# A causal mask moved from TensorE matmuls to a GpSimd select, and normalisation moved ahead of the low halves in two later stages of a two-layer transformer kernel

## The chip, the cores and the metric

One core of one Trainium2 chip runs the whole program in one launch. The metric is device microseconds (us) from start to end of an execution. The profile comes from one more execution under the hardware profiler. Engines are named as the profile names them: PE is TensorE's matmuls, PEld its weight loads, DVE is VectorE, ACT ScalarE, POOL GpSimd, SP SyncE.

## What is computed

```python
h = layernorm(x) * (1 + ca) + sa
x = x + ga * causal_attention(h)      # B=2, T=2048, C=256, 16 heads of 16, 32 rotary dimensions, softmax over keys <= query
h = layernorm(x) * (1 + cb) + sb
x = x + gb * experts(h)               # 8 experts of 3 layers; softmax over tokens, the 2 largest of 8
h = layernorm(x) * (1 + ca1) + sa1
z = softmax(h @ W_A.T * 0.25, over tokens)
x = x + ga1 * ((toeplitz(z) @ v) @ W_O + b_O)  # out[i] = sum over j <= i of z[i - j] * v[j], for each head
h = layernorm(x) * (1 + cb1) + sb1
x = x + gb1 * sigmoid(xr @ W_r) * (relu(xk @ W_k)**2 @ W_v)   # xr, xk mix a token with the one before it
```

All inputs and the output are float32; the scale and shift vectors come from a small conditioning product.

## The kernel before

Six stages follow one another with a barrier between them: start (projections), attention, route, experts, mix and tail. `N` = 8 chunks of 512 tokens, `NB` = 2 batches of `NCH` = 4 chunks. Each engine has its own instruction list, written by hand, and engines meet at semaphores alone.

**Attention** (`phase_attention`) runs 8 units `u` (4 groups of 4 heads, times 2 batches). A unit has 40 steps: for each chunk `qc` of 512 queries, in the order 3, 2, 1, 0 (unit 0: 2, 3, 1, 0), all blocks `kb` of 128 keys up to the diagonal. In the last four steps of a chunk the key block lies on the diagonal, at `t = kb - 4*qc` = 0 to 3, and the query columns shrink to 512, 384, 256 and 128. Of the 40 steps 16 are diagonal. In a step PE does, for each of two head pairs `f`, six score matmuls of half the array's rows each (two at a time, lines L916 and L920), and on a diagonal step four more of 128 columns (L925) that add -1e30 to the future keys of the block, as mask times identity in bf16. ACT takes the exponential (L963) into one of two buffers `pr`. PE then multiplies the step before with the values (`weighted`, L898); it waits there for `exp_done` of both `f`:

```python
for s in range(NS):
    ahead(u, s, 0)
    ...
    scores(s, 0)
    scores(s, 1)
    ...
        weighted(grp, b, s - 1)
    ahead(u, s, 7)
```

**Maxima.** The softmax's shift is the true row maximum, found in advance: PE computes the score products a second time, transposed (`maxima`, L863), into three banks used as a ring; DVE reduces each (L999, on the diagonal L996, with a mask of its own) and frees the bank. When a chunk of queries is done, its maxima are gathered (DVE L1006), turned by PE (L874), scaled by DVE (L1010), and sent by four DMAs of the SP queue (L837) into the row of `sqk` that scores of that chunk read (`shift_ld`). `schedule()` decides at build time at which place of which step (0 to 7) each maximum and each turn is issued: it plays the steps through with a cost in ns for each operation, among them 106 ns for the mask of each `f`, and holds maxima back until it takes a bank to be free. At place 0 of a chunk's first step it puts as many maxima as fit until 5400 ns (`FETCH`) after that chunk's turn.

POOL in attention first splits the experts' weights into f16 high and low parts (24 times: fetch L771, L784, L787, store L790), then stores each finished chunk (L799), fills zeros (L803), loads and stores the sums' inverses.

**Route** (`phase_route`): for each chunk PE projects the attention output (L1354), DVE adds it to `x` (L1176), takes statistics (L1183, L1187), ACT the root (L94), DVE normalises (L1197), PE transposes (L1364), ACT modulates (L1307), PE computes gate logits (L1388) and transposes back (L1395), ACT copies the f16 high halves (L1332), DVE subtracts for the low halves (L1204, `low`). **Mix** (`phase_mix`) has the same flow (DVE add L1723, statistics, normalise L1744, low halves L1752; PE transposes L1853, products for `z` L1862 and `v` L1870). It then takes the softmax of `z` over tokens (DVE maximum L1757, ACT exponential L1802), POOL scales it and splits it into f16 halves (L1679, L1683, L1685, 16 partitions of 2048), SP stores it and reads it back as Toeplitz tiles (L1713), and 32 units of matmuls follow (L1899, L1901). In both stages PE's list for chunk n is: outputs of n + 2, transposes of n + 1, products of n.

## Time and profile before

| | us |
|---|---|
| median of 3 runs (range) | 1815.13 (1814.72 to 1819.74) |
| profiled execution: time, span of its instructions | 1819.15, 1817.5 |
| PE, DVE, ACT, POOL busy | 1551.9, 1154.6, 893.4, 362.4 |
| attention, from 192.1 to 1048.9 | 856.8 |
| route up to the softmax, from 1064.0 to 1158.8 | 94.8 |
| mix up to its first unit, from 1472.0 to 1560.5 | 88.5 |

Busy times are unions of an engine's instructions; a granted clock of 1.00 is TensorE's full 2.4 GHz. The rows by stretch further down are those of attention, route, mix and, last, of attention's unit 3 alone. The profiled execution took 4.0 us more than the median. Averages over the span mix six stages, so a change is read in its own stage.

### The profile page before, as it was taken

What the parts mean: (1) busy time and instruction counts of PE and PEld (TensorE: products, weight loads), DVE (VectorE), ACT (ScalarE), POOL (GpSimd) and SP (SyncE); (2) the same over time, 40 slices, a digit from 0 to 9 for tenths busy, and PEclk for the clock granted to TensorE, in tenths of its full rate; (3) what the DMA queues carried; (4) which work ended last, traced back from release to release, by engine and by line L of the source; (5) the groups of instructions that cost most, each with busy time, mean ns of one, the idle gap of its engine ahead of it and who ended that gap; (6) DMA issues with size and microseconds to landing.
All of it is one profiled execution on the core that took longest, in us unless ns stands there. A gap on an engine that the chain in (4) does not pass through costs nothing. (4 is left out here: it accounts for less than half of the span.)

```text
span 1817.5 us, 34523 instructions
## 1 busy us (share of the span) xinstructions
PE 1551.9 (85%) x13070; PEld 851.3 (47%) x13070; DVE 1154.6 (64%) x3222; ACT 893.4 (49%) x1272; POOL 362.4 (20%) x432
## 2 busy tenths in 40 slices
PE   7994989999999999999999958401899967988898
PEld 5451334444444434444343334200787744666776
DVE  3746888888888888888888138400556666211775
ACT  2430456666666666666666714300676734201443
POOL 2471782000000000000000022175111001510011
PEclk9995889999999999999999989655999979999999
DMA  8378442304040130404010045024777600776011
GB/s 301 110 215 207 137 134 77 66 29 86 17 95 5 45 70 29 86 15 93 8 42 15 30 148 205 16 106 94 89 82 78 77 7 2 245 282 231 12 35 47
DMA packets 102197, 166.59 MB, mean 92 GB/s; under 512 B 23596, under 2 KB 72492, under 8 KB 100884
## 3 DMA queue, kind: packets, MB, share of 16 engines
q1 hardware_dynamic: 83124, 113.15, 26.6%
q0 software_dynamic: 16112, 47.59, 8.3%
q10 hardware_dynamic: 2800, 3.64, 0.6%
q8 instruction: 109, 1.79, 0.5%
q14 instruction: 52, 0.43, 0.1%
HBM read 107.76 MB, written 56.47 MB: 90 GB/s over the span
## 5 line engine op out<-in xcount | busy, mean ns | idle before, releaser
L963 ACT ACTIVATE at_pr<-ps 128x1024 f32<-128x1024 f32 (+3 forms) x640 | 542.5, 894 | 296.6 <-PE ps L920 175.9
L999 DVE TENSOR_REDUCE at_mx<-ps 128x1 f32<-128x512 f32 x768 | 483.2, 684 | 87.2 <-PE ps L863 84.1
L920 PE MATMUL ps<-bq,bk 64*128 64x512 f16 (+3 forms) x1280 | 287.1, 346 | 0.0
L996 DVE CUSTOM_DVE_ANT_0 at_seen<-ps,later 128x384 bf16<-128x384 f32 (+3 forms) x512 | 228.4, 487 | 20.6 <-PE ps L863 18.9
L916 PE MATMUL ps<-sqk 64*128 64x512 f16 (+3 forms) x1280 | 215.3, 348 | 0.1
L916 PE MATMUL ps<-at_sqk 64*128 64x512 f16 (+3 forms) x1280 | 207.5, 345 | 0.5 <-ACT at_pr L963 0.2
L863 PE MATMUL ps<-sqk 64*128 64x512 f16 (+3 forms) x640 | 173.8, 375 | 22.7 <-PEq L543 11.4
L863 PE MATMUL ps<-at_sqk 64*128 64x512 f16 (+3 forms) x640 | 157.9, 350 | 1.1 <-DVE at_mx L999 0.7
L898 PE MATMUL ps<-at_pr,at_vl 128*32 128x512 f32 (+3 forms) x1280 | 150.0, 541 | 0.1
L898 PE MATMUL ps<-at_pr,vl 128*32 128x512 f32 (+3 forms) x1280 | 150.0, 541 | 0.0
L863 PEld LDWEIGHTS ps<-sqk 64*128 64x128 f16 x640 | 45.5, 94 | 164.9 <-DVE at_mx L999 89.6
L920 PEld LDWEIGHTS ps<-bq,bk 64*128 64x128 f16 x1280 | 98.4, 94 | 39.6 <-issue 0.2
L1517 PE MATMUL ps<-ex_id,ex_xr 128*128 128x128 f16 x312 | 25.5, 228 | 105.7 <-DMA ex_xr<-d_rows 104.8
L1899 PE MATMUL ps<-mi_vhl,mi_tz 128*128 128x512 f16 (+15 forms) x512 | 96.0, 284 | 15.5 <-DMA mi_tz<-d_z 15.4
L1541 PE MATMUL ps<-ex_hh,exw 128*128 128x256 f16 x624 | 105.2, 274 | 0.9 <-DVE ex_hl L1597 0.9
L863 PEld LDWEIGHTS ps<-at_sqk 64*128 64x128 f16 x640 | 42.9, 93 | 132.8 <-DVE at_mx L999 70.4
L916 PEld LDWEIGHTS ps<-at_sqk 64*128 64x128 f16 x1280 | 77.0, 94 | 54.0 <-ACT at_pr L963 23.0
L916 PEld LDWEIGHTS ps<-sqk 64*128 64x128 f16 x1280 | 82.8, 95 | 40.4 <-ACT at_pr L963 8.2
L925 PE MATMUL ps<-mask,ident 64*128 64x128 bf16 x1024 | 95.9, 216 | 0.0
L1557 ACT ACTIVATE ex_xt<-ps 128x1024 f16<-128x1024 f16 x39 | 40.0, 1025 | 103.2 <-PE ps L1517 102.9
L1901 PE MATMUL ps<-mi_vhl,mi_tz 128*128 128x256 f16 (+15 forms) x512 | 87.8, 225 | 0.0
L1541 PE MATMUL ps<-ex_hl,exw 128*128 128x256 f16 x312 | 85.3, 274 | 0.1
(277 smaller groups left out, 2351.2 us busy)
## 6 DMA issues: line engine op xcount, KB each, us to landing
mi_tz<-d_z SPq DMA_DIRECT2D x32, 1024.0 KB, 7.1
ex_xr<-d_rows SPq DMA_DIRECT2D x39, 256.0 KB, 8.7
d_rows<-at_nil POOLq DMA_DIRECT2D x31, 322.0 KB
d_va<-st_va SPq DMA_DIRECT2D x8, 1024.0 KB, 4.3
d_o<-at_oc POOLq DMA_DIRECT2D x32, 256.0 KB, 2.4
at_pw<-in_w POOLq DMA_DIRECT2D x24, 256.0 KB, 3.3
d_w<-at_ph POOLq DMA_DIRECT2D x24, 256.0 KB, 2.4
exw<-d_w SPq DMA_DIRECT2D x8, 768.0 KB, 13.5
```

Source lines behind the costliest of these rows:

```text
L863: pe.matmul(ps[:, MAXB + slot % RING, 0:hi_ - lo], g.sqk[b][half[r], 0, i, 0, qb * P:(qb + 1) * P], g.sqk[b][half[r], 1, i, 0, lo:hi_], st ...
L898: ins = pe.matmul(ps[32 * h:32 * h + 32, O, off:CH], g.vl[b][:, kb, 32 * h:32 * h + 32], pr[:, n % 2, h // 2, h % 2, off:CH], start=(kb == 0),
L916: pe.matmul(ps[:, 2 * f + r, off:CH], g.sqk[b][half[r], 1, f, part, k], g.sqk[b][half[r], 0, f, part, q], start=part == 0, stop=False)
L920: ins = pe.matmul(ps[:, 2 * f + r, off:CH], g.bk[half[r], b, k], g.bq[half[r], b, q], start=False, stop=t < 0)
L925: ins = pe.matmul(ps[:, 2 * f + r, off:off + P], g.ident2[half[r], m, :], g.mask2[half[r], m, :], start=False, stop=m == 1)
L963: act.activation(pr[:, n % 2, f, :, off:CH], ps[:, 2 * f:2 * f + 2, off:CH], ACT.Exp, scale=INV_SCALE).then_inc(exp_done[f], 1)
L996: ins = dve.tensor_tensor_reduce(seen[:, turn, r, 0:n], src, g.later[:, CH - n:CH], 1.0, LOWEST, ALU.add, ALU.max, dst)
L999: ins = dve.tensor_reduce(dst, src, AX.X, ALU.max)
L1541: ins = pe.matmul(out(l, cc)[:, o, :], lhs, rhs, start=(i == 0), stop=(i == len(parts) - 1))
L1557: act.activation(xt[:, cc % 2], turning(cc), ACT.Copy).then_inc(xt_ready, 1)
L1899: pe.matmul(out[:, :, d * HD:C], tz[:, x, 0, w], vhl[:, :, tiles, h * HD:(h + 1) * HD], start=(d == 0), stop=False)
L1901: ins = pe.matmul(out[:, 0, d * HD:C], tz[:, x, 1, w], vhl[:, 0, tiles, h * HD:(h + 1) * HD], start=False, stop=(d == NT - 1))
```

## The change

It has three parts.

1. **Attention.** The mask matmuls go. The exponential runs on unmasked scores, and POOL then sets the future keys of each diagonal block of `pr` to zero by `affine_select` (128 partitions x 2 x 128), one for each `f`: 256 in all. `weighted` waits for `masked` on diagonal steps. POOL's list is rewritten around that: the weight splits are spread over the chunks of units 0 to 2 (`SPLITS`), zeros are filled in the long chunks, stores of a chunk come early in the next. The planner loses its 106 ns entries, and so its table changes. The constants `mask2` and `ident2`, their loads and their casts in the start stage go.
2. **Route and mix.** `normalise(n + 2)` stands ahead of `low(n)` in DVE's list.
3. **Mix.** The maximum of `z` is taken chunk by chunk; `Z_SCALE` goes into the sum; ACT instead of POOL writes the high halves, beside POOL's scaling.

```diff
-            pool.dma_start(msk32[:, :, :], g.i["mask2"]).then_inc(late_ld, 16)
-            pool.dma_start(idn32[:, :, :], g.i["ident2"]).then_inc(late_ld, 16)
...
-                dve.tensor_copy(g.gb0[:, 1, :], craw[0:VROWS, 0, 1, 1, :])
-                dve.wait_ge(late_ld, 16 * (NLATE + 1))
-                dve.tensor_copy(g.ident2[:, :, :], idn32[:, :, :])
-                dve.tensor_copy(g.mask2[:, :, :], msk32[:, :, :]).then_inc(gate_used, 1)
+                dve.tensor_copy(g.gb0[:, 1, :], craw[0:VROWS, 0, 1, 1, :]).then_inc(gate_used, 1)
...
-    INV_STEP = 24
+    INV_STEP = 14
+    SPLITS = {(0, 2): 6, (0, 3): 7, (0, 1): 2, (1, 3): 4, (1, 2): 3, (2, 3): 2}
...
-                        if i % 3 == 0 and t >= 0:
-                            rows[:] = [max(rows) + 106] * 2
...
-            pool.wait_ge(ld[1], loaded(0, 1))
-            fetch(0)
-            for n in range(3 * E):
+            def split(n):
...
+            def store(u, i):
+                grp, b = divmod(u, NB)
+                qc = ORDER[u][i]
+                pool.wait_ge(out_moved, u * NCH + i + 2)
+                pool.dma_start(g.d_o[grp][:, b * T + qc * CH:b * T + (qc + 1) * CH], oc[:, i % 2, :])\
+                    .then_inc(o_stored[i % 2], 16)
+
...
+            def mask_step(u, n, t):
+                d = u * NS + n
+                cut = slice(t * P, (t + 1) * P)
+                for f in range(2):
+                    pool.wait_ge(exp_done[f], d + 2)
+                    block_ = pr[:, n % 2, f, :, cut]
+                    pool.affine_select(block_, block_, pattern=[[0, 2], [1, P]], compare_op=ALU.is_ge, fill=nought, base=0,
+                                       channel_multiplier=-1).then_inc(masked[f], 1)
+
+            pool.wait_ge(ld[1], loaded(0, 1))
+            fetch(0)
+            n_split = 0
+            nought = pool.to_reg(0.0)
+
             def body(grp, b, last):
+                nonlocal n_split
                 u = index(grp, b)
                 for i, qc in enumerate(ORDER[u]):
-                    pool.wait_ge(out_moved, u * NCH + i + 2)
...
+                    if qc and (u or i):
+                        store(*divmod(u * NCH + i - 1, NCH))
+                    if i == 0 and u:
+                        load_sums(u - 1)
+                    if i == 1 and u:
+                        store_inverses(u - 1)
+                    if qc:
+                        for x in range(1 + (qc == 3)):
+                            fill(u * NCH + sum(1 + (q == 3) for q in ORDER[u][:i] if q) + x)
+                    for n in range(SPLITS.get((u, qc), 0)):
+                        split(n_split)
+                        n_split += 1
+                    for t in range(TPC):
+                        mask_step(u, ENDS[u][qc] - TPC + 1 + t, t)
+                        if qc == 0 and t == 0:
+                            store(u, i - 1)
+                if last:
+                    store(u, NCH - 1)
...
-                    pe.wait_ge(exp_done[f], u * NS + n + 2)
+                    if kb >= TPC * qc:
+                        pe.wait_ge(masked[f], u * NT + diagonals(u, n) + 1)
+                    else:
+                        pe.wait_ge(exp_done[f], u * NS + n + 2)
...
-                                        start=False, stop=t < 0)
-                    if t >= 0:
-                        for m in range(2):
-                            for r in range(2):
-                                ins = pe.matmul(ps[:, 2 * f + r, off:off + P], g.ident2[half[r], m, :],
-                                                g.mask2[half[r], m, :], start=False, stop=m == 1)
+                                        start=False, stop=True)
...
                     add(n + 2)
                     statistics(n + 2)
+                    normalise(n + 2)
                 low(n)
-                if n + 2 < N:
-                    normalise(n + 2)
...
-                pool.tensor_scalar(z[:, b, :], z[:, b, :], zrec[:, b:b + 1], Z_SCALE, ALU.mult, ALU.mult).then_inc(zn_ready, 1)
-                pool.wait_ge(zn_ready, b + 1)
                 if b:
                     pool.wait_ge(z_st[b - 1], 32)
-                pool.tensor_copy(zhl[:, 0, :], z[:, b, :]).then_inc(zh_ready, 1)
+                pool.tensor_scalar(zn[:, :], z[:, b, :], zrec[:, b:b + 1], None, ALU.mult).then_inc(zn_ready, 1)
+                pool.wait_ge(zn_ready, b + 1)
                 pool.wait_ge(zh_ready, b + 1)
-                pool.tensor_tensor(zhl[:, 1, :], z[:, b, :], zhl[:, 0, :], ALU.subtract).then_inc(zl_ready, 1)
+                pool.tensor_tensor(zhl[:, 1, :], zn[:, :], zhl[:, 0, :], ALU.subtract).then_inc(zl_ready, 1)
...
-            def largest(b):
-                dve.wait_ge(z_ready, NCH * (b + 1))
-                dve.tensor_reduce(nmax[:, b:b + 1], z[:, b, :], AX.X, ALU.max, negate=True).then_inc(nmax_ready, 1)
+            def largest(n):
+                b, it = n // NCH, n % NCH
+                dve.wait_ge(z_ready, n + 1)
+                dve.tensor_reduce(zmax[:, b, it:it + 1], z[:, b, it * CH:(it + 1) * CH], AX.X, ALU.max).then_inc(zmax_ready, 1)
+                if it == NCH - 1:
+                    dve.wait_ge(zmax_ready, n + 1)
+                    dve.tensor_reduce(nmax[:, b:b + 1], zmax[:, b, :], AX.X, ALU.max, negate=True).then_inc(nmax_ready, 1)
 
             def inverse(b):
                 dve.wait_ge(exp_ready, b + 1)
+                dve.tensor_scalar(zsum[:, b:b + 1], zsum[:, b:b + 1], 1.0 / Z_SCALE, None, ALU.mult).then_inc(sum_ready, 1)
+                dve.wait_ge(sum_ready, b + 1)
                 dve.reciprocal(zrec[:, b:b + 1], zsum[:, b:b + 1]).then_inc(rec_ready, 1)
...
                 if n + 2 < N:
                     add(n + 2)
                     statistics(n + 2)
+                    normalise(n + 2)
                 low(n)
-                if n + 2 < N:
-                    normalise(n + 2)
-                if n == NCH - 1:
-                    largest(0)
+                largest(n)
                 if n == NCH:
                     inverse(0)
-            largest(1)
             inverse(1)
...
+            def highs(b):
+                act.wait_ge(rec_ready, b + 1)
+                if b:
+                    act.wait_ge(z_st[b - 1], 32)
+                act.activation(zhl[:, 0, :], z[:, b, :], ACT.Copy, scale=zrec[:, b:b + 1]).then_inc(zh_ready, 1)
...
                     exps(0)
+                    highs(0)
             exps(1)
+            highs(1)
```

How the table moves. PE's list (`L863`, after the change `L897`, are maxima; `L874`/`L908` the turn; `L916`/`L953` and `L920`/`L957` the scores; `L925` the mask; `L898`/`L935` the values). Before, at the end of unit 1, from the turn of unit 2's first chunk (first row) to that chunk's first scores (last row):

```order
L874 MATMUL ps<-ident,at_mm 128x128
L863 MATMUL ps<-sqk 128x512 x2
L916 MATMUL ps<-at_sqk 128x384 x4
L920 MATMUL ps<-bq,bk 128x384 x2
L925 MATMUL ps<-mask,ident 128x128 x4
L863 MATMUL ps<-sqk 128x512
...
L925 MATMUL ps<-mask,ident 128x128 x4
L863 MATMUL ps<-sqk 128x128
L898 MATMUL ps<-at_pr,at_vl 32x256 x4
L916 MATMUL ps<-sqk 128x512 x2
```

The same place after the change, again from the turn (second row) to the first scores (last row):

```order
L953 MATMUL ps<-at_sqk 128x256 x2
L908 MATMUL ps<-ident,at_mm 128x128
L897 MATMUL ps<-sqk 128x512 x2
L953 MATMUL ps<-at_sqk 128x256 x2
...
L897 MATMUL ps<-sqk 128x512 x2
L953 MATMUL ps<-at_sqk 128x128 x4
...
L935 MATMUL ps<-at_pr,at_vl 32x256 x4
L897 MATMUL ps<-sqk 128x128 x2
L897 MATMUL ps<-sqk 128x512 x4
L897 MATMUL ps<-sqk 128x128 x2
L953 MATMUL ps<-sqk 128x512 x2
```

The turn stood in front of step 37; it now stands inside step 38, behind half of its first scores. Between it and the next unit's first scores lay the rest of three steps (37 to 39) and 12 maxima, spread out among them; now it is the rest of two, and 12 maxima, eight of them in one piece directly ahead of those scores.

DVE's list in route, before:

```order
L1187 BN_AGGR ro_mv<-ro_st 128x2 x4
L1204 TENSOR_TENSOR ro_rows<-ps,ro_rows 128x4x256
L1193 RECIPROCAL ro_rs<-ro_sd 128x4
L1197 TENSOR_SCALAR ro_hn<-x,ro_mv,ro_rs 128x256 x4
L1228 TENSOR_REDUCE ro_cmax<-ro_lg 8x1
```

and after:

```order
L1219 BN_AGGR ro_mv<-ro_st 128x2 x4
L1225 RECIPROCAL ro_rs<-ro_sd 128x4
L1229 TENSOR_SCALAR ro_hn<-x,ro_mv,ro_rs 128x256 x4
L1236 TENSOR_TENSOR ro_rows<-ps,ro_rows 128x4x256
L1259 TENSOR_REDUCE ro_cmax<-ro_lg 8x1
```

The subtraction (L1204, now L1236) has changed places with the reciprocal and the four normalisations.

## Rows read from the trace of the kernel before


**Rows 1.** The page's costliest groups, line L925: out<-in, times, busy us and mean ns, idle

```profile
L925 PE MATMUL ps<-mask,ident 64*128 64x128 bf16 x1024 | 95.9, 216 | 0.0
```

**Rows 2.** Stretch, its us, busy PE, PEld, DVE, ACT, POOL, granted clock, DMA share, GB/s

```profile
192.10:1048.90 856.80, 848.42 (x8676) 349.85 (x8676) 685.69 (x2033) 557.50 (x673) 123.26 (x168) 0.99 0.23 56
1064.00:1158.80 94.80, 69.23 (x316) 44.40 (x317) 62.34 (x151) 35.26 (x47) 22.41 (x13) 0.86 0.40 144
1472.00:1560.50 88.50, 66.28 (x257) 40.20 (x257) 49.65 (x145) 33.80 (x53) 7.90 (x3) 0.84 0.12 41
526.50:632.70 106.20, 105.91 (x1096) 44.01 (x1094) 89.77 (x266) 69.56 (x85) 5.57 (x10) 1.00 0.23 49
```

**Rows 3.** PE's timeline over a full step and the diagonal one after it

```profile
608.47 1.06 PE L898 MATMUL ps<-at_pr,at_vl 128*32 128x512 f32 x8
...
611.25 1.07 PE L898 MATMUL ps<-at_pr,at_vl 128*32 128x512 f32 x8
...
613.12 0.48 PE L925 MATMUL ps<-mask,ident 64*128 64x128 bf16 x4
...
614.49 1.07 PE L898 MATMUL ps<-at_pr,at_vl 128*32 128x512 f32 x8
```

**Rows 4.** PE's timeline in a step of 128 columns

```profile
417.44 0.28 PE L925 MATMUL ps<-mask,ident 64*128 64x128 bf16 x4
417.55 0.22 PE L863 MATMUL ps<-sqk 64*128 64x128 f16 x1
```

**Rows 5.** The timeline: exponentials of diagonal blocks and the value products that wait for them

```profile
386.29 1.09 ACT L963 ACTIVATE at_pr<-ps 128x512 f32<-128x512 f32 x2 [1.38 <-PE ps L925]
...
388.04 0.64 PE L898 MATMUL ps<-at_pr,at_vl 128*32 128x256 f32 x8
...
411.07 1.94 ACT L963 ACTIVATE at_pr<-ps 128x1024 f32<-128x1024 f32 x2 [1.28 <-PE ps L925]
...
414.00 1.06 PE L898 MATMUL ps<-at_pr,at_vl 128*32 128x512 f32 x8
```

**Rows 6.** Groups of POOL's instructions, shapes apart

```profile
L1689 POOL TENSOR_TENSOR x<-x,mi_bias 128x256 f32<-128x256 f32 x32 | 21.9, 716 | 0.0
...
L1156 POOL MEMSET ro_zeros<- 128x256 f32 x1 | 0.3, 303 | 0.0
```

**Rows 7.** The timeline: POOL released by ACT, in the tail stage

```profile
1717.79 0.60 ACT L2086 ACTIVATE tl_kr<-ps 128x512 f32<-128x512 f32 x1 [6.31 <-PE ps L2147]
...
1718.54 1.04 POOL L1959 TENSOR_TENSOR tl_ka<-tl_kr 128x512 f32<-128x512 f32 x1 [12.86 <-ACT tl_kr L2086]
```

**Rows 8.** The timeline at the end of unit 1: turn, and unit 2's first scores

```profile
412.01 0.33 PE L874 MATMUL ps<-ident,at_mm 128*128 128x128 f32 x1
...
418.94 0.39 PE L916 MATMUL ps<-sqk 64*128 64x512 f16 x2
```

**Rows 9.** The timeline in unit 0's step 12: DVE's reductions while PE waits for banks

```profile
233.49 1.29 DVE L999 TENSOR_REDUCE at_mx<-ps 128x1 f32<-128x512 f32 x2 [0.27 <-PE ps L863]
...
235.48 1.29 DVE L999 TENSOR_REDUCE at_mx<-ps 128x1 f32<-128x512 f32 x2 [0.27 <-PE ps L863]
```

**Rows 10.** PE's waits in route, 1060 to 1160 us: us in all, times, longest

```profile
PE ps L1364 <- DVE ro_hn L1197: 15.4, 8, 3.9
```

**Rows 11.** DVE's timeline in route: low halves, normalising beside POOL and without it

```profile
1088.79 1.23 DVE L1204 TENSOR_TENSOR ro_rows<-ps,ro_rows 128x1024 f16<-128x1024 f32 x1 [2.03 <-ACT ro_rows L1332]
...
1090.13 3.41 DVE L1197 TENSOR_SCALAR ro_hn<-x,ro_mv,ro_rs 128x256 f32<-128x256 f32 x4
...
1111.40 1.38 DVE L1197 TENSOR_SCALAR ro_hn<-x,ro_mv,ro_rs 128x256 f32<-128x256 f32 x4
```

**Rows 12.** PE's waits in mix, 1465 to 1562 us: us in all, times, longest

```profile
PE ps L1853 <- DVE mi_hn L1744: 21.9, 8, 4.1
```

**Rows 13.** PE's timeline in mix: one product at either clock

```profile
1505.80 2.54 PE L1862 MATMUL ps<-mi_ht,mi_wa 128*16 128x512 f32 x4
...
1515.94 1.89 PE L1862 MATMUL ps<-mi_ht,mi_wa 128*16 128x512 f32 x4
```

More of the change, by code:

```diff
@@ L175, in phase_start @@
         sc = sb("sc", [P, 2, KT, NB])
-        msk32 = sb("msk32", [P, 2, P])
-        idn32 = sb("idn32", [P, 2, P])
         wkv = sb("wkv", [P, KT, DC])
@@ L210, in phase_start @@
         NST = 7
-        NLATE = 10
+        NLATE = 8
         NBANK = 6
@@ L595, in turned, with diagonals @@
         return v * UNIT + (turn_slot(v, m) + 1 if m + 1 < NCH else UNIT)
+    def diagonals(u, n):
+        return sum(kb >= TPC * qc for qc, kb in STEPS[u][:n])
     def width(v, k):
@@ L739, in phase_attention @@
         pv_done = [sem(f"pv_done{f}") for f in range(2)]
+        masked = [sem(f"masked{f}") for f in range(2)]
         O, MAXB = 4, 5
@@ L791, in _, with fill @@
                     .then_inc(pw_st[x], 16)
+            def fill(n):
+                at = n * NIL
+                end = min(at + NIL, ALL)
+                pool.dma_start(d_fill[:, at:end], nil[:, 0:end - at]).then_inc(filled, 16)
+            def store(u, i):
[4 more added lines that the diff above has]
+                    .then_inc(o_stored[i % 2], 16)
@@ new lines, in load_sums, with store_inverses @@
+            def load_sums(u):
+                for x in range(2):
+                    pool.wait_ge(o_stored[x], 16 * (NCH // 2) * (u + 1))
+                pool.dma_start(sums[:, u % 2, :], sums_of(g, *divmod(u, NB))).then_inc(sums_ld, 16)
+            def store_inverses(u):
+                pool.wait_ge(inv_ready, u + 1)
+                pool.dma_start(inverses_of(g, *divmod(u, NB)), inv[:, u % 2, :]).then_inc(inv_st, 16)
+            def mask_step(u, n, t):
[6 more added lines that the diff above has]
+                                       channel_multiplier=-1).then_inc(masked[f], 1)
@@ L793, in body @@
+            pool.wait_ge(ld[1], loaded(0, 1))
+            fetch(0)
+            n_split = 0
+            nought = pool.to_reg(0.0)
             def body(grp, b, last):
+                nonlocal n_split
                 u = index(grp, b)
                 for i, qc in enumerate(ORDER[u]):
-                    pool.wait_ge(out_moved, u * NCH + i + 2)
-                    row = g.d_o[grp] if isinstance(grp, int) else \
-                        g.d_o[bass.ds(grp, 1)].rearrange("g p n -> (g p) n")
-                    pool.dma_start(row[:, b * T + qc * CH:b * T + (qc + 1) * CH], oc[:, i % 2, :])\
-                        .then_inc(o_stored[i % 2], 16)
@@ L801, in body @@
-                    at = (u * NCH + i) * NIL
-                    end = min(at + NIL, ALL)
-                    pool.dma_start(d_fill[:, at:end], nil[:, 0:end - at]).then_inc(filled, 16)
-                if not last:
-                    for x in range(2):
-                        pool.wait_ge(o_stored[x], 16 * (NCH // 2) * (u + 1))
-                    pool.dma_start(sums[:, u % 2, :], sums_of(g, grp, b)).then_inc(sums_ld, 16)
-                    pool.wait_ge(inv_ready, u + 1)
-                    pool.dma_start(inverses_of(g, grp, b), inv[:, u % 2, :]).then_inc(inv_st, 16)
+                    if qc and (u or i):
+                        store(*divmod(u * NCH + i - 1, NCH))
@@ L1650, in phase_mix @@
         zhl = sb("zhl", [NH, 2, T], F16)
+        zn = sb("zn", [NH, T])
         zero = sb("zero", [NH, 2, P], F16)
         nmax = sb("nmax", [NH, NB])
+        zmax = sb("zmax", [NH, NB, NCH])
+        zmax_ready, sum_ready = sem("zmax_ready"), sem("sum_ready")
         zsum = sb("zsum", [NH, NB])
@@ L2212, in adaln_two_layers @@
         g.ident = sb("ident", [P, P])
-        g.ident2 = sb("ident2", [P, 2, P], BF16)
-        g.mask2 = sb("mask2", [P, 2, P], BF16)
         g.later = sb("later", [P, CH])
@@ L2269, in constants @@
     count = np.broadcast_to(np.arange(NCK), (P, NCK))
-    mask2 = np.tile(mask.reshape(2, 64, P).transpose(1, 0, 2), (2, 1, 1))
-    ident2 = np.tile(np.eye(P).reshape(2, 64, P).transpose(1, 0, 2), (2, 1, 1))
-    return {"ident": np.eye(P), "mask2": mask2, "later": later, "ident2": ident2, "cs": cs, "lower": lower,
+    return {"ident": np.eye(P), "later": later, "cs": cs, "lower": lower,
             "falling": falling, "count": count, "lane": i[:, None]}
```

## The prediction

> **What bounds the kernel now.** I read the page first, then the busy time by stretch, and from there the timeline and the waits of the stretches that the change touches. Averages over the span don't decide: the mask lives in attention, the reordering in route and mix.
>
> In attention PE is the bound. In a steady unit of 106.2 us it is busy for 105.91, at a granted clock of 1.00, against 89.77 for DVE, 69.56 for ACT and 5.57 for POOL [rows 2]. Work taken from PE there comes off the time, as long as nothing else gets in the way. The page puts 95.9 us of busy time on the mask matmuls [rows 1], but that is no price: a busy time holds the overlap with the neighbours. In route and mix PE is busy for 69.23 of 94.80 us and 66.28 of 88.50, at a mean clock of 0.86 and 0.84 [rows 2]: there an order can be what costs, and the waits say which.
>
> **Part 1a, the mask matmuls.** Their price is read from the distance between two value products. An undiagonal step lasts 611.25 - 608.47 = 2.78 us, the diagonal one behind it 614.49 - 611.25 = 3.24 [rows 3]; the diagonal one has the same 512 columns and four maxima as well. So the mask costs at most 0.46 us a step. In a narrow step four mask matmuls start 0.11 us ahead of what follows [rows 4], 0.22 a step for both `f`. I take 0.30, since three of four diagonal steps are narrower than the one in rows 3, and keep 0.22 and 0.46 as bounds. A unit has 16 such steps, so 4.8 us (3.5 to 7.4), and eight units 38.4.
>
> **Part 1b, where it goes.** Not all of it arrives. The planner sees shorter steps, and puts the turn of the next unit's first chunk later, with eight maxima in one piece ahead of the first scores. Before, from turn to scores took 418.94 - 412.01 = 6.93 us [rows 8], with PE busy throughout. Now the turn stands behind most of one step (some 2.2 us by rows 3, less for fewer columns) and three steps' masks are gone (0.75): PE has 4.0 us of work there. But the 12 maxima need DVE, and where PE waits for banks DVE takes 235.48 - 233.49 = 1.99 us for four [rows 9]: 12 take 6.0, and since the first are under way at the turn, I take 5.8. PE then stands for 1.8 us at each boundary into units 2 to 7. Unit 1's boundary and unit 0's start lose less; there DVE already paces. Unit 0 gives 3.6 us, unit 1 4.5, the other six 4.8 - 1.8 = 3.0 each: **26.1 us**.
>
> **Part 1c, the selects.** 256 of them on POOL, which is busy for 123.26 of 856.80 us in attention [rows 2]; even at 1 us each there is room in the sum. What counts is the chain: exponential, select, value product. No affine select stands in the trace. A two-input POOL instruction of the same 128x256 elements takes 716 ns, and a fill of them 303 [rows 6]. A select reads one input and computes a comparison; it lies between, and I take 0.50 us, with 0.30 and 0.74 as the near ends and 1.1 as the far one (nothing in the trace excludes a slow form). Handing over from ACT to POOL takes 1718.54 - 1718.39 = 0.15 us [rows 7], handing back to PE I take at 0.05, so a value product has to come 0.70 us behind the exponential. How much it does today: in the third diagonal step the exponential ends at 387.38 and the product starts at 388.04, 0.66 us later; in the first diagonal step of a unit's last chunk the two are 414.00 - 413.01 = 0.99 us apart [rows 5]. Other diagonal steps have 0.9 to 1.9 by the same reading. The masks of the step behind stood in these gaps and go, and so do that step's maxima where the planner moves them, so I reckon with 0.44 at the shortest and 0.6 in the mean for the third diagonal step (a stall of about 0.08 a time, 32 times) and 0.45 for the first of the last chunk (0.25, 8 times): **+4.6 us**. A stall costs PE in full, since its list is in order and the next scores stand behind the value products. At 0.30 us a select this is nothing, at 0.74 it is 18.
>
> The Trainium skill, GPSIMD Engine Reference, section 3.1, gives about 1.8 cycles an element for a tight loop without data-dependent branching; as an estimate, 256 elements at 1.2 GHz would take 0.38 us, and the stalls would be near nothing instead of 4.6. By its figure for the two-input form, 2.6, they would take 0.55, against the 0.716 of rows 6, so the page runs low for a short instruction here.
>
> The splits of the experts' weights, fills and stores that now stand between the selects cost nothing by the planned places: each group of splits lies in the undiagonal part of a chunk, where no select is due. If one runs over, the first diagonal block waits, about 1 us each time; that is inside the range. The start stage's loads and casts of the mask are not on its path.
>
> **Part 2, route.** PE waits 15.4 us for the normalised chunk in 8 waits [rows 10]. The order explains it: `low` needs PE's last products and ACT's copy (DVE L1204 begins 2.03 us late), and normalising stands behind it with nothing of that kind to wait for [rows 11]. With the change it is done before. The first two waits, 3.2 us by the same view, belong to the pipeline's start and stay; 12.2 can go. But beside POOL's product DVE's normalising takes 3.41 us instead of 1.38 [rows 11], and `low` then comes later and frees its bank later. I take **-9 us** (-2.5 to -12).
>
> **Part 3, mix.** The same: 21.9 us in 8 waits [rows 12], 5.4 of them the first two, so 16.5 can go. In addition the clock: a product takes 2.54 us at the half clock and 1.89 at the full one [rows 13], and PE starts such a chunk at 1.2 GHz behind a wait of 4 us; without the waits some 3 us come back. Against it, DVE has about 7.1 us of work a chunk beside PE's 7.0, so it becomes the bound at the margin (+2), and normalising beside POOL's scaling and ACT's high halves, now a 2048-element pass in ACT's list, cost some 3.5. The maximum by chunk takes a pass over 2048 elements off the end and spreads it. **-14 us** (-6 to -18).
>
> **Sum.** -26.1 + 4.6 - 9 - 14 = -44.5. The profiled execution took 1819.15, so it would take 1774.6; it lies 4.0 above the median, and against the median of 1815.13 the forecast is **1771 us**.
>
> **Rivals.**
> - A, dearer selects (0.74 to 0.95 us each). Stalls of 18 to 24 us or more in place of 4.6, third diagonal steps first: 1784 to 1795. For it: rows 6 price an elementwise POOL instruction of that size at 0.716, and a select has two free dimensions. Chance 0.16.
> - B, the other side: the select is so slow that PE waits for it in every diagonal step. Each step then pays for the price of two selects less what the step lasts, narrow steps first, since POOL handles both `f` one after the other in a step of 1.3 to 3 us. At 1.05 us the stalls eat the whole 44.5 + 4.6; at 1.1 us they are about 58, hence 1815.1 - 49.1 + 58 = 1824, and each further 0.1 us adds 13 to 25. It decides from 1.05 us on. Against it: all plain POOL instructions in rows 6 are below 0.75 at this size. The same section of the Trainium skill gives about 12 cycles an element where a loop branches on data, which would be an estimated 2.6 us and this rival in full; a select need not branch. Chance 0.08.
> - C, attention gives next to nothing: the boundaries and the maxima hold PE everywhere, because DVE at 89.77 of 106.2 us [rows 2] is the next bound and paces whenever maxima bunch. Only route and mix come: 1815.1 - 23 = 1792. Against it: DVE keeps 16 us of room a unit. Chance 0.09.
> - D, all of it arrives: masks at 0.46 with no wait at a boundary (8 times 7.4 less some 8) or route and mix at their far ends: 1750 to 1756. Chance 0.09.
> - The forecast, 1760 to 1783 for itself: chance 0.58.
>
> **Numbers.** 0.3% of the time, about what a measurement of this kernel can tell from no change, is 5.4 us. Faster by more: forecast, A, C, D, 0.88 after the part of A and C that falls short; same 0.04, a select near 1 us; slower 0.08. The range leaves out B and the outer ends of the others, 0.16 together: 1751 to 1798.
>
> **What would show it.** In a steady unit PE's span of 106.2 falls to about 103; selects show a mean of 0.5 us; PE's waits for POOL's `pr` sum to about 5 us, mostly in third diagonal steps; at each unit boundary PE waits for DVE's maxima, 1.8 us. In route and mix the waits of the transposes shrink from 15.4 and 21.9 to a few us beyond the first two, and the mean clock of mix rises from 0.84. The forecast is wrong if a select takes 0.75 us or more, if a unit is still 105 us or more, or if the transposes' waits are as long as before with `low` no longer ahead of them.

## The result, and the profile after

The changed kernel takes 1796.9 us against 1817.4 (medians of 4 runs each), a ratio of 0.988 (95% interval 0.984 to 0.991). A second sitting gave 0.990 (0.987 to 0.993). So it is faster, by 20.5 us where 44.5 were forecast.

Busy times of the page, of the profiled execution of 1798.60 us:

```profile
PE 1531.2 (85%) x12046; PEld 818.9 (46%) x12046; DVE 1155.0 (64%) x3230; ACT 895.0 (50%) x1274; POOL 468.7 (26%) x684
```

The same stretches as [rows 2], in the same columns (stretch, its us, busy PE, PEld, DVE, ACT, POOL, granted clock, DMA share, GB/s): attention, route, mix, unit 3 alone:

```profile
192.90:1044.00 851.10, 833.26 (x7652) 318.69 (x7652) 683.93 (x2033) 556.61 (x673) 226.03 (x424) 0.98 0.23 56
1058.30:1146.00 87.70, 67.09 (x320) 44.93 (x320) 61.92 (x152) 34.71 (x47) 23.29 (x13) 0.89 0.44 154
1465.30:1541.90 76.60, 62.57 (x257) 38.70 (x257) 54.01 (x153) 35.24 (x54) 9.49 (x2) 0.83 0.13 47
524.60:630.50 105.90, 103.69 (x968) 39.85 (x966) 89.43 (x266) 69.29 (x85) 18.44 (x42) 1.00 0.24 49
```

PE lost 20.7 us of busy time, 15 of them in attention, yet attention itself is only 5.7 us shorter: unit 3, with 128 matmuls fewer, lasts 105.9 us instead of 106.2. Route and mix gave 7 and 12 us in these stretches. By stage, each from its first to its last matmul (attention from its first exponential), before and after: attention 852.8 and 847.1; route 105.3 and 98.1; experts 201.9 and 208.4; mix 201.7 and 187.3; the rest within 1 us. The sum, -20.8, is the difference of the two executions (1819.15 and 1798.60) to 0.3 us.

The 6.5 us that experts lost lie within that stage's own spread, and its code is unchanged: in the twelve further traces it lasted 185 to 212 us, whatever the kernel. PE's extra waits are for the gathered rows' transfers (110.1 us in the page of after, 104.8 before; some 92 of them come ahead of the stage's first matmul in both).

The select, and what waited for it (groups of the page: busy us, mean ns, idle before):

```profile
L814 POOL TENSOR_SCALAR_AFFINE_SELECT at_pr<-at_pr 128x256 f32<-128x256 f32 x256 | 103.0, 407 | 444.9 <-ACT at_pr L995 441.8
...
L935 PE MATMUL ps<-at_pr,at_vl 128*32 128x512 f32 (+3 forms) x1280 | 150.0, 540 | 1.8 <-POOL at_pr L814 1.6
```

A select takes 0.41 us, between the two rows of [rows 6], and PE's visible waits for it are 1.6 us in all. Visible waits alone don't prove it, but a1 below does: the selects did not eat the gain. PE's timeline at the end of unit 3 (start us, us, engine, line) shows where it went:

```profile
621.81 0.33 PE L908 MATMUL ps<-ident,at_mm 128*128 128x128 f32 x1
...
623.63 0.85 PE L935 MATMUL ps<-at_pr,at_vl 128*32 128x384 f32 x8 [0.62 <-POOL at_pr L814]
...
625.64 0.23 PE L897 MATMUL ps<-sqk 64*128 64x128 f16 x2
626.18 0.82 PE L897 MATMUL ps<-sqk 64*128 64x512 f16 x3 [0.31 <-DVE at_mx L1031]
627.35 0.39 PE L897 MATMUL ps<-sqk 64*128 64x512 f16 x1 [0.35 <-DVE at_mx L1031]
627.95 0.23 PE L897 MATMUL ps<-sqk 64*128 64x128 f16 x1 [0.21 <-DVE at_mx L1031]
628.55 0.23 PE L897 MATMUL ps<-sqk 64*128 64x128 f16 x1 [0.37 <-DVE at_mx L1031]
628.65 0.39 PE L953 MATMUL ps<-sqk 64*128 64x512 f16 x2
```

From the turn (L908) to the next unit's first scores (L953) pass 6.84 us, with a step less of work in them than in the 6.93 of [rows 8]: PE walks through the eight maxima at DVE's pace. This boundary is the longest of the seven, though. The first takes 6.23 us and the other five 6.15, as at the end of unit 5:

```profile
833.91 0.33 PE L908 MATMUL ps<-ident,at_mm 128*128 128x128 f32 x1
...
840.06 0.61 PE L953 MATMUL ps<-sqk 64*128 64x512 f16 x2
```

The distances between value products, step by step, agree: up to step 37 unit 3 gains 3.56 us on the kernel before, and in step 38 alone it loses 3.51; in units 2, 4 and 5 the two are 4.15 and 3.4 to 4.65. The 0.69 us more at the end of unit 3 go with the wait for POOL at 623.63: there the store of the chunk before (L796), which stands between two blocks' selects, starts 1.78 us after the first of them ends. In the other seven units it starts 0.31 us after it. What held it up here is not shown.

```profile
622.15 0.56 POOL L796 DMA_DIRECT2D d_o<-at_oc  x1 [1.78 <-issue]
...
622.71 1.63 POOL L814 TENSOR_SCALAR_AFFINE_SELECT at_pr<-at_pr 128x256 f32<-128x256 f32 x4
```

In route and mix the waits that answer to [rows 10, 12]:

```profile
PE ps L1395 <- DVE ro_hn L1229: 8.3, 5, 3.9
```

```profile
PE ps L1897 <- DVE mi_hn L1777: 13.7, 3, 8.3
```

Both are down. The first two waits of each stage stay (3.0 and 5.4 us), so of the 12.2 and 16.5 us that could go, 6.9 and 8.2 went. What is left in mix is one wait of 8.3 us. Its neighbourhood in the timeline:

```profile
1517.02 2.00 ACT L1845 ACTIVATE mi_zhl<-mi_z,mi_zrec 16x2048 f16<-16x2048 f32 x1 [0.39 <-DVE mi_zrec L1800]
1517.09 5.45 POOL L1715 TENSOR_SCALAR mi_zn<-mi_z,mi_zrec 16x2048 f32<-16x2048 f32 x1 [52.90 <-DVE mi_zrec L1800]
...
1520.84 1.28 ACT L94 ACT_TABLE_LOAD   x1
1522.13 0.30 ACT L94 ACTIVATE mi_sd<-mi_mv,eps 128x4 f32<-128x4 f32 x1
1522.46 0.18 DVE L1773 RECIPROCAL mi_rs<-mi_sd 128x4 f32<-128x4 f32 x1 [2.44 <-ACT mi_sd L94]
1522.62 4.04 POOL L1718 TENSOR_TENSOR mi_zhl<-mi_zn,mi_zhl 16x2048 f16<-16x2048 f32 x1
1522.68 5.11 DVE L1777 TENSOR_SCALAR mi_hn<-x,mi_mv,mi_rs 128x256 f32<-128x256 f32 x4
1527.84 1.97 PE L1897 MATMUL ps<-ident,mi_hn 128*128 128x128 f32 x8 [8.28 <-DVE mi_hn L1777]
```

The last root (L94) stands behind ACT's high halves (L1845), and the normalising that needs it takes 5.11 us beside POOL's subtraction instead of 1.38. It is not slower throughout: one of the four instructions takes 4.14 us, from the start of POOL's 4.04 us to behind its end, and the other three 0.40 each. All 32 normalisings of the stage (shortest, median and longest in ns):

```profile
L1777 DVE TENSOR_SCALAR mi_hn<-x,mi_mv,mi_rs x32: 400/406/4140, 1470.3 to 1527.4; 128x256 f32<-128x256 f32 x32
```

POOL is there that late because its scaling took 5.45 us.

### The profile page after: what moved, and what is told of

The parts are those of the page before. It is cut to its first block and busy times, and to the rows that moved or that the text cites. A ratio compares the mean times of both kernels' runs of the same rounds, so it can differ in the third digit from the quotient of the medians.

```text
span 1796.8 us, 32741 instructions
## 1 busy us (share of the span) xinstructions
PE 1531.2 (85%) x12046; PEld 818.9 (46%) x12046; DVE 1155.0 (64%) x3230; ACT 895.0 (50%) x1274; POOL 468.7 (26%) x684
## 5 line engine op out<-in xcount | busy, mean ns | idle before, releaser
L957 PE MATMUL ps<-bq,bk 64*128 64x512 f16 (+3 forms) x1280 | 291.1, 347 | 0.0
L814 POOL TENSOR_SCALAR_AFFINE_SELECT at_pr<-at_pr 128x256 f32<-128x256 f32 x256 | 103.0, 407 | 444.9 <-ACT at_pr L995 441.8
L953 PE MATMUL ps<-sqk 64*128 64x512 f16 (+3 forms) x1280 | 210.9, 352 | 0.7 <-ACT at_pr L995 0.7
L953 PE MATMUL ps<-at_sqk 64*128 64x512 f16 (+3 forms) x1280 | 203.5, 347 | 1.5 <-ACT at_pr L995 1.3
L897 PE MATMUL ps<-sqk 64*128 64x512 f16 (+3 forms) x640 | 177.7, 378 | 25.6 <-DVE at_mx L1031 13.4
L897 PE MATMUL ps<-at_sqk 64*128 64x512 f16 (+3 forms) x640 | 163.2, 351 | 4.2 <-DVE at_mx L1031 3.7
L935 PE MATMUL ps<-at_pr,at_vl 128*32 128x512 f32 (+3 forms) x1280 | 150.0, 540 | 1.8 <-POOL at_pr L814 1.6
L935 PE MATMUL ps<-at_pr,vl 128*32 128x512 f32 (+3 forms) x1280 | 150.2, 541 | 0.1
L897 PEld LDWEIGHTS ps<-sqk 64*128 64x128 f16 x640 | 46.3, 95 | 174.1 <-DVE at_mx L1031 89.2
L1548 PE MATMUL ps<-ex_id,ex_xr 128*128 128x128 f16 x312 | 25.6, 229 | 110.2 <-DMA ex_xr<-d_rows 110.1
L957 PEld LDWEIGHTS ps<-bq,bk 64*128 64x128 f16 x1280 | 100.5, 95 | 41.6 <-issue 0.5
L897 PEld LDWEIGHTS ps<-at_sqk 64*128 64x128 f16 x640 | 44.0, 93 | 146.2 <-DVE at_mx L1031 73.8
L1943 PE MATMUL ps<-mi_vhl,mi_tz 128*128 128x512 f16 (+15 forms) x512 | 94.7, 281 | 14.3 <-DMA mi_tz<-d_z 14.0
L953 PEld LDWEIGHTS ps<-at_sqk 64*128 64x128 f16 x1280 | 78.1, 94 | 55.7 <-ACT at_pr L995 24.3
L953 PEld LDWEIGHTS ps<-sqk 64*128 64x128 f16 x1280 | 84.4, 95 | 41.8 <-ACT at_pr L995 8.9
L1626 DVE CAST ex_hh<-ex_hf 128x512 f16<-128x512 f32 x78 | 33.6, 430 | 85.9 <-ACT ex_hf L1605 84.8
## 6 DMA issues: line engine op xcount, KB each, us to landing
exw<-d_w SPq DMA_DIRECT2D x8, 768.0 KB, 12.2
```

The costliest lines, as they stand in the source:

```text
L814: pool.affine_select(block_, block_, pattern=[[0, 2], [1, P]], compare_op=ALU.is_ge, fill=nought, base=0, channel_multiplier=-1).then_inc( ...
L897: pe.matmul(ps[:, MAXB + slot % RING, 0:hi_ - lo], g.sqk[b][half[r], 0, i, 0, qb * P:(qb + 1) * P], g.sqk[b][half[r], 1, i, 0, lo:hi_], st ...
L935: ins = pe.matmul(ps[32 * h:32 * h + 32, O, off:CH], g.vl[b][:, kb, 32 * h:32 * h + 32], pr[:, n % 2, h // 2, h % 2, off:CH], start=(kb == 0),
L953: pe.matmul(ps[:, 2 * f + r, off:CH], g.sqk[b][half[r], 1, f, part, k], g.sqk[b][half[r], 0, f, part, q], start=part == 0, stop=False)
L957: ins = pe.matmul(ps[:, 2 * f + r, off:CH], g.bk[half[r], b, k], g.bq[half[r], b, q], start=False, stop=True)
L1943: pe.matmul(out[:, :, d * HD:C], tz[:, x, 0, w], vhl[:, :, tiles, h * HD:(h + 1) * HD], start=(d == 0), stop=False)
```

## The experiments

Theories: **1**, the moved table of maxima costs what the masks gave; **2**, the chain of exponential, select and value product does; **3**, DVE's reductions set the pace, whatever PE does. Times are those of one profiled execution, by stage, unless an interval is given. `att` is attention as above, `unit` the mean of units 2 to 6, `flow` mix up to its first unit, from its first matmul. Where two traces have the same code in a stage, they differ by up to 0.4 us in attention (847.1 and 847.1; 832.2 and 831.8) and 1.4 in the flow (70.8 and 72.2), so differences of 1 or 2 us in the flow are weak.

| kernel | att | unit | route | flow |
|---|---|---|---|---|
| before | 852.8 | 106.2 | 105.3 | 89.9 |
| changed; again | 847.1; 847.1 | 105.8; 105.8 | 98.1; 94.7 | 78.0; 78.2 |
| a1_no_select | 847.2 | 106.3 | 95.8 | 78.4 |
| a2_mask_left_out | 837.8 | 104.4 | 98.6 | 87.9 |
| a3_old_table | 842.4 | 104.9 | 95.1 | 77.8 |
| a4_fetch3600 | 832.2 | 103.4 | 95.4 | 77.1 |
| b1_fetch2400_twoop | 839.0 | 103.5 | 96.8 | 73.9 |
| b2_select_twice | 851.8 | 105.6 | 96.0 | 77.1 |
| b3_order_alone | 830.3 | 103.3 | 96.6 | 75.9 |
| b4_slack300 | 836.8 | 104.1 | 96.9 | 70.8 |
| c1_short_masked | 830.6 | 103.5 | 99.5 | 88.7 |
| c2_short_no_mask | 808.4 | 100.7 | 100.6 | 89.5 |
| c4_combined | 831.8 | 103.4 | 94.8 | 72.2 |

**a1_no_select**, the selects left out of the changed kernel.

```diff
-                    if kb >= TPC * qc:
-                        pe.wait_ge(masked[f], u * NT + diagonals(u, n) + 1)
-                    else:
-                        pe.wait_ge(exp_done[f], u * NS + n + 2)
+                    pe.wait_ge(exp_done[f], u * NS + n + 2)
...
-                        mask_step(u, ENDS[u][qc] - TPC + 1 + t, t)
```

> The changed kernel without its selects: the value products wait for the exponential alone, so future keys are not masked. Attention, from the first exponential to the last matmul, lasts 847.1 us in the changed kernel and 852.8 in the one before. Theory 1, the moved table costs what the masks gave (about 3.5 us at each of 7 unit ends, which stays here): 840 to 845. Theory 2, the chain exponential, select, value product costs it: 815 to 828. Theory 3, the DVE's reductions bound a unit whatever PE does: 845 to 847.

847.2 us, the same as with them. Theory 2 falls for this table. That it is not even the 840 to 845 of theory 1 left theory 3 open. The equality is partly a cancelling: units 2 to 4 are 0.3 to 1.2 us longer without the selects, unit 0 and unit 7 shorter.

**a2_mask_left_out**, in the kernel before.

```diff
-                                        start=False, stop=t < 0)
-                    if t >= 0:
-                        for m in range(2):
-                            for r in range(2):
-                                ins = pe.matmul(ps[:, 2 * f + r, off:off + P], g.ident2[half[r], m, :],
-                                                g.mask2[half[r], m, :], start=False, stop=m == 1)
+                                        start=False, stop=True)
```

> The kernel before, with the mask matmuls left out and nothing in their place (no mask at all), and its table of maxima unchanged. It prices the masks alone. If they are worth the 4.8 us a unit of the prediction, attention lasts 852.8 - 38 = 814; if they are worth what the step-by-step comparison shows up to step 37 (3.6 a unit), 824; theory 3 (DVE bounds): 848 or more.

837.8: the masks were worth 15.0 us in all, 1.8 a unit, which none of the three figures had. By the distances between value products of unit 3, leaving them out saves 0.20 to 0.22 us in five of the 16 diagonal steps, 0.11 in six and nothing (0.03 at most) in five; in the step of [rows 3], 0.11. The timeline shows why. A wide diagonal step of the kernel before:

```profile
559.62 1.29 DVE L999 TENSOR_REDUCE at_mx<-ps 128x1 f32<-128x512 f32 x2 [0.73 <-PE ps L863]
559.86 0.54 PE L920 MATMUL ps<-bq,bk 64*128 64x512 f16 x2
560.07 0.43 PE L925 MATMUL ps<-mask,ident 64*128 64x128 bf16 x4
560.37 0.33 PE L863 MATMUL ps<-at_sqk 64*128 64x384 f16 x1
```

and the same one with the masks left out:

```profile
554.12 1.29 DVE L994 TENSOR_REDUCE at_mx<-ps 128x1 f32<-128x512 f32 x2 [0.73 <-PE ps L863]
554.36 0.54 PE L920 MATMUL ps<-bq,bk 64*128 64x512 f16 x2
554.87 0.33 PE L863 MATMUL ps<-at_sqk 64*128 64x384 f16 x1
```

With or without L925, the next maximum (L863) starts 0.51 us behind L920, and 0.75 behind the start of DVE's two reductions, each of which takes 0.65: it waits for the bank that the first of them frees. PE's list is in order, so this mask lay under that wait. The busy rows hide it (the ends of matmuls are modelled, and their rows run into each other).

**a3_old_table**, the changed kernel with the planner's 106 ns put back.

```diff
                             rows[r] = now + ticks(w)
+                        if i % 3 == 0 and t >= 0:
+                            rows[:] = [max(rows) + 106] * 2
```

> The changed kernel with the table of the kernel before (the planner keeps its 106 ns for each mask, so turns and maxima stand where they stood). Theory 1 (moved table): attention 822 to 828 instead of 847.1. Theory 2 (selects) and theory 3 (DVE): 843 to 848.

842.4, between the expectations. With a2 it gives one way to split the result: masks gone, on the old table, -15.0; selects in their place, with POOL's rewritten list, +4.6; the moved table, +4.7. The sum is the -5.7 that was measured. The parts are not independent: without selects the moved table costs 847.2 - 837.8 = 9.4 (a1 and a2), and the selects then nothing. In a steady unit the moved table gains 2.7 us on a3 in the first 38 distances between value products and loses 3.2 to 4.0 in the last two.

**a4_fetch3600**.

```diff
-    HEAD_STEP, AHEAD, FETCH, SLACK = 6, 2, 5400, 100
+    HEAD_STEP, AHEAD, FETCH, SLACK = 6, 2, 3600, 100
```

> The changed kernel with FETCH 3600 instead of 5400: four maxima instead of seven stand directly ahead of a unit's first scores, the turn stays where the change put it. Theory 1, if the clump of maxima is what costs: 834 to 838 for attention (the shift's transfer lands about 1.6 us before the scores start now). If the late turn itself, with its transfer, is what costs: 844 to 847. Theories 2 and 3: 846 to 848.

832.2, 14.9 us less than the changed kernel. Directly ahead of the first scores stand five maxima instead of eight, and from the turn to the scores pass 830.25 - 826.04 = 4.21 us, where the same boundary took 6.15:

```profile
826.04 0.33 PE L908 MATMUL ps<-ident,at_mm 128*128 128x128 f32 x1
...
830.25 0.50 PE L953 MATMUL ps<-sqk 64*128 64x512 f16 x2
```

FETCH acts on every chunk, but the gain is at the unit's end: in units 2 and 5 the last two distances between value products shrink by 2.5 and 3.3 us, and the 38 before them grow by 0.6 together. So it is the maxima bunched there that cost, and the moved table is good inside a unit and was bad at its end. The kernel before was not run with FETCH 3600; whether it would gain as well stays open.

**b1_fetch2400_twoop**. FETCH 2400, and in mix:

```diff
-                pool.tensor_scalar(zn[:, :], z[:, b, :], zrec[:, b:b + 1], None, ALU.mult).then_inc(zn_ready, 1)
+                pool.tensor_scalar(zn[:, :], z[:, b, :], zrec[:, b:b + 1], 1.0, ALU.mult, ALU.mult).then_inc(zn_ready, 1)
```

> Two edits in stages apart, each read in its own stage. Attention: FETCH 2400, so one maximum instead of four (3600) or seven (5400) stands directly ahead of a unit's first scores. If the clump is all that costs, attention falls below the 832.2 us of FETCH 3600, to 828 to 831; if at 3600 the first scores already wait for the shift's transfer, it stays within 1 us of 832 or gets longer, since PE then waits with nothing to do. Mix (187.4 us in the changed kernel, first to last matmul): POOL's scaling in a form with two operations (times the sum's inverse, times 1.0). If the form is what makes it 5.44 us instead of 1.97, it takes about 2 us again and mix gets 1 to 3 us shorter; if it is ACT reading the same rows beside it, nothing changes.

839.0: units 2 to 6 are as with 3600, but unit 0 is 5.2 us longer and unit 1 1.2, and no run shows why; a shorter FETCH gives nothing more. In mix the second operation, which multiplies by one, makes POOL's scaling 2.8 times as fast (groups of POOL's instructions, this kernel):

```profile
L1715 POOL TENSOR_SCALAR mi_zn<-mi_z,mi_zrec 16x2048 f32<-16x2048 f32 x2 | 3.9, 1967 | 72.4 <-DVE mi_zrec L1800 72.4
```

and that of the changed kernel:

```profile
L1715 POOL TENSOR_SCALAR mi_zn<-mi_z,mi_zrec 16x2048 f32<-16x2048 f32 x2 | 10.9, 5438 | 73.0 <-DVE mi_zrec L1800 73.0
```

ACT's high halves ran beside it in both, so it is the form; the flow is 4 us shorter, and the one long normalising is gone (1.67 us for the four).

**b2_select_twice**, FETCH 3600, two selects for each block, and `highs(0)` behind the last root.

```diff
+                                       channel_multiplier=-1).then_inc(again, 1)
+                    pool.wait_ge(again, 2 * (u * NT + TPC * ORDER[u].index(STEPS[u][n][0]) + t) + f + 1)
+                    pool.affine_select(block_, block_, pattern=[[0, 2], [1, P]], compare_op=ALU.is_ge, fill=nought, base=0,
...
                 if n + 2 < N:
                     root(n + 2)
+                if n == NCH + 1:
+                    highs(0)
```

> Attention: FETCH 3600 and every select issued twice, so each block's mask takes about 0.85 us instead of 0.41. If the chain of exponential, select and value product has no slack left (theory 2), 64 steps with the shortest gap each lose about 0.4 to 0.8 us: 832.2 + 25 to 50. If slack covers it, under 5 us. The prediction's own sum (0.44 to 1.2 us of slack) gives some 18 to 25. Mix: ACT's high halves of the first batch moved behind the last root. If PE's stall of 8.3 us there is ACT's queue (exponential, high halves, then the root), it falls by about 2 us and mix by 1 to 3 us; if the Toeplitz loads, which wait for the high halves, come later and bound the units, mix gets 2 to 5 us longer instead.

851.8, so 19.6 us for the second select. PE's visible waits for POOL are 20.1 us in 38 waits, 13.9 of them in third diagonal steps, which is where the prediction's rival A (18 us at 0.74 a select, 24 at 0.95) had put them. Mix's flow, 77.1, did not move against a4, which has 77.1 too: the root now came early, but the normalising ran into POOL's long scaling and the subtraction behind it, and took 6.86 us.

**b3_order_alone**, FETCH 3600 without selects, and mix with the changed order only (maximum, scaling and high halves of `z` as before).

> Attention: FETCH 3600 without selects (future keys not masked), beside the 832.2 us with them. If the selects are hidden on this table as on the changed one (847.2 without, 847.1 with): within 2 us. If the clump hid them there: 5 to 15 us less. Mix: the changed order of normalising alone, with the maximum, scaling and high halves of z as in the kernel before. If the order gives the whole gain of mix (14.4 us): 187 to 189; if the high halves on ACT and the maximum by chunk give a part: 190 to 196.

830.3, so with FETCH 3600 the selects cost 1.9 us: nothing in a steady unit, 0.7 at the end of unit 3, the rest in unit 7. The flow is 75.9, 2 us better than the changed kernel: the order gives all of mix's gain and more (89.0, the mean of the four traces with the old order, to 75.9), and the work on `z` gave some 2 back. With the other form of the scaling (b1, 73.9) that loss is gone.

**b4_slack300**, FETCH 3600, SLACK 300, and both edits of mix.

> Attention: FETCH 3600 and SLACK 300, so the planner issues a maximum up to 0.3 us before a bank is free by its reckoning. If the planner's wide margin leaves DVE idle (it is idle for 14 us of a unit's 103.3), units get shorter, 101 to 103; if PE then waits for banks, 103.3 to 105. Mix: both edits of the other two kernels, the form with two operations and the later high halves: the sum of their gains if they act on separate waits.

836.8, 4.6 us longer than a4: of the two cases expected, the one in which PE waits for banks (a unit of 104.1). Its visible waits for DVE's reductions grew only from 10.4 to 12.0 us, so that cause is likely and not shown. Flow 70.8: with the scaling short, the later high halves give 3 us more (1.7 by c4, whose mix is the same).

**c1_short_masked** and **c2_short_no_mask**: the kernel before, and a2, with DVE's reductions of off-diagonal blocks over half their columns, so that the shift is not the true maximum.

```diff
-                        ins = dve.tensor_reduce(dst, src, AX.X, ALU.max)
+                        ins = dve.tensor_reduce(dst, src[:, 0:n // 2], AX.X, ALU.max)
```

> The kernel before, masks in, but DVE's 512-column reductions of the maxima read only their first half (the shift is then not the row's true maximum). It frees banks about 0.33 us earlier, 96 times a unit. If PE's work is what a unit of 106.2 us consists of, it stays within 0.5 us; if PE waits for banks in ways that its busy row does not show, it falls to 102 to 105. Its second use is as the reference for the next kernel.

> The same short reductions, and the mask matmuls left out as in the earlier kernel of that kind (old table, no selects). With full reductions the masks were worth 106.2 - 104.4 = 1.8 us a unit. If the rest of their time lay under waits for a bank that DVE frees, the difference to the kernel with short reductions and masks rises to 3 to 4 us a unit (16 steps by 0.22, the spacing of rows 4). If the masks are worth 1.8 by themselves (they run on the half of the array that is free), it stays at 1.8.

With masks and short reductions a unit takes 103.5 us instead of 106.2. Unit 3 of c1, in the columns of [rows 2]:

```profile
509.45:613.00 103.55, 103.55 (x1098) 42.77 (x1095) 66.96 (x265) 69.38 (x84) 5.55 (x10) 1.00 0.24 51
```

Nothing of PE's work was changed, so of the 105.91 us in which PE is "busy" in [rows 2], at least 2.4 were waits for DVE; PE's row is full in both. Without masks a unit takes 100.7, so the masks are now worth 2.8 us a unit instead of 1.8, just short of the 3 to 4 expected: some of the mask's time lay under DVE's, and without that the price is 0.18 a step (0.17 to 0.22 in 14 of the 16), not 0.30. Theory 3 is right in part: DVE, idle for 16 us of a unit, still holds PE. It does so in diagonal steps and in three others near a chunk's start; in the rest of unit 3 the distances between value products are the same with short reductions as with full ones.

**c3_changed_again** and **c4_combined** (FETCH 3600, the form with two operations, the later high halves), five rounds each on one chip.

> The changed kernel once more, for an interval, a second profile, and a comparison on the same chip with the next one: ratio to the kernel before 0.983 to 0.992. Attention 847 us as before; experts anywhere from 192 to 212.

> The changed kernel with FETCH 3600, the form with two operations for POOL's scaling, and the high halves of z behind the last root. By stages: attention 832 (15 us less than the changed kernel), mix 7 us less up to its first unit. So 20 to 23 us below the changed kernel, a ratio to the kernel before of 0.970 to 0.980.

Ratios to the kernel before: 0.990 (0.987 to 0.993) and 0.975 (0.971 to 0.979); medians 1784.9 and 1757.4 us, against 1805.2. The combined kernel gives 48 us instead of 20. Of the 27.5 between the two medians, 20 to 23 were expected. In the profiled executions, 21.8 us apart, attention gives 15.3 and mix 4.3, experts take 4.4, and the tail stage, whose code is the same, gives 5.5: its granted clock is 1.00 in c4 and 0.95 in c3. It lasted 132.8 to 132.9 us in b1, b3 and c4 and 136.6 to 138.4 in the other traces, and no run shows why.

## Why the prediction was wrong

**Part 1a is the step that failed.** It priced the mask at 0.30 us a step, 38.4 in all; a2 measured 0.11 a step, 15.0 in all. The upper bound of 0.46 came from subtracting two unlike steps [rows 3]; leaving the masks out shortens that diagonal step by 0.11. The lower, 0.22 from the spacing in [rows 4], is about PE's own work (0.18 with short reductions) and was taken as a floor. It was none: in a list worked in order, work is free where the next instruction waits for another engine anyway. The premise beneath, that a unit is PE's work because PE is busy 105.91 of 106.20 us [rows 2], is what the short reductions refute. Rival C, at a chance of 0.09, came nearest: attention gives next to nothing because DVE holds PE, 1792 forecast, 1796.9 measured. It looked for this where maxima bunch; a2 shows it at single banks in diagonal steps as well. That the time lies in the stated range of 1751 to 1798 is luck: the forecast's own mechanism does not lead there, and its own sign of being wrong, a unit of 105 us or more, came true.

**Part 1b** saw the right mechanism in the right place, from the order alone: 5.8 us from turn to scores were forecast, 6.15 measured. What it made of them was too much. It let 38.4 - 26.1 = 12.3 us be lost by the move; against a3 the move cost 4.7, because the new table also gains 2.7 us inside a steady unit, which the sum had not. Against what the new table can do, the bunched maxima cost 14.9 (a4). So in attention the terms are: masks 38.4 forecast and 15.0 measured, the move -12.3 and -4.7, the selects -4.6 and -4.6.

**Part 1c.** A select was forecast at 0.50 us and takes 0.41; forecast were 4.6 us in all, and measured 4.6 on the old table, 1.9 with FETCH 3600 and nothing in the changed kernel. That the first agrees to the digit is chance. On the old table a steady unit loses 0.37 us, nearly all of it where the longest chunk ends, and the rest is lost at the end of unit 3 and in unit 7; these are not the places that part 1c had, and POOL's rewritten list is in the figure too. The chain itself was right: made slow enough (b2), it stalls most where part 1c had its shortest gaps, in third diagonal steps and in the first of the last chunk (2.8 us in 8 waits). The Trainium skill's best case of 1.8 cycles an element (GPSIMD Engine Reference, section 3.1) gave an estimated 0.38 us; the trace's 407 ns is near it. The same section of the Trainium skill has 12 cycles an element for loops that branch on data, 2.56 us by estimate; the trace's 407 ns rules that out for this select.

**Part 2**: -9 forecast, -7.2 in the first pair of traces. Four traces of the old order spread from 98.6 to 105.3 us (mean 101.0) and ten of the new from 94.7 to 98.1 (mean 96.0), so the order is worth about 5, and some 2 of the 7 were chance. The waits behind the first two fell from 12.2 to 5.3 us.

**Part 3**: -14 forecast, -14.4 measured, 11.9 of it in the flow. The other 2.5, in the 32 units that follow, are within the spread there (109 to 114 us over the traces), so the close agreement is partly chance. The sum hides two errors: the order alone gives 13, with no loss to DVE as a bound, and the rework of `z` costs some 2 because a form of instruction that the trace of before did not show took 5.44 us. Of the 11.9, 8.2 are waits; the other 3.7 are PE's own busy time in the flow (67.67 us before, 63.95 after), about the 3 us that part 3 expected of the clock. Before, the transposes (L1853) took 1.97 us, the half clock, in five of eight chunks; after, in three, the first two and the last, the ones that PE still waited for. Its sign for that did not show: the mean granted clock of the stretch is 0.83, not above 0.84. Nor did part 3 read the wait rightly: ahead of both products' chunks in [rows 13] PE waited 2.48 us, not 4, and one ran at each clock.

Of the 24 us between forecast and result, attention is 15.8 (21.5 forecast, 5.7 measured), route 1.8, and 6.5 are what experts lost in the profiled pair. In the second sitting the gain was 20 again, with 192.0 us for experts in its profiled execution; how long they took in the kernel before was not profiled there. In rival D the sums don't lead to the 1750 to 1756 it states: its masks alone would give 1741, its far ends of route and mix alone 1764.

## What to carry to other kernels

Price a removed instruction by what its engine does next, not by its busy time: if the next one waits for another engine anyway, the work was free up to the length of that wait. A busy row near 100% does not show that; shortening the other engine's work does. And when a planner's costs change, look first at where its list bunches work in front of something that the rest waits for, and read more than one such place: here one boundary of seven was 0.7 us off the others.

## What the runs showed of the hardware

POOL's `tensor_scalar` on 16x2048 float32 took 5438 ns with one multiplication by a column of scalars and 1967 ns with a second multiplication, by 1.0. An `affine_select` of 128x2x128 float32 in place took 407 ns. DVE's normalising of four 128x256 tiles took 5.11 us beside POOL's subtraction of 16x2048 and 1.38 alone; the whole difference is in one of the four instructions, which ended 0.16 us behind POOL's. In [rows 11] it is the same: the 3.41 us are three instructions of 0.41 and one of 2.44, which began 0.12 us behind POOL's product of 2.40 and ended 0.15 behind it.
